# A three-layer recurrent scan as one unrolled stream at lags of 18 and 36 steps, with layer 0's input projections reading x in place

## What is computed

```
def step(h, x_t):                       # layer 0: gated
    fused = sigmoid(concat([x_t, h]) @ w_W + w_b)
    hidden_state, output_state = split(fused, 2)
    memory_state = x_t @ wx_W + wx_b + hidden_state * (h @ wh_W + wh_b)
    h_new = output_state * h + (1 - output_state) * tanh(memory_state)
x = x + layer0(x)                       # the scan over t gives h_1 .. h_512
x = x + layer1(x)                       # h_t = tanh(x_t @ Wx + b + h_{t-1} @ Wh)
x = x + layer2(x)                       # the same form
x = x + attention(x)                    # 16 heads, causal, an extra image token
```

## Time and profile before

| | us |
|---|---|
| median of 3 runs | 4057.07 |
| the profiled execution, own time | 4053.96 |
| its span in the trace | 4052.3 |
| TensorE busy | 3869.1 (95%) |
| VectorE busy | 2335.6 (58%) |
| ScalarE busy | 1066.0 (26%) |
| GpSimd busy | 159.7 (4%) |

### The profile page before, as it was taken

The page is one execution under the profiler, slowest core; times in us unless marked ns, Lnnn a source line. Parts: engine busy times, 40 slices in busy tenths (PEclk is TensorE's granted clock), DMA queues, the critical chain, the costliest instruction groups (busy, mean ns, idle before and its releaser), DMA issues. The chain is left out here.

```text
span 4052.3 us, 172362 instructions
## 1 busy us (share of the span) xinstructions
PE 3869.1 (95%) x78452; PEld 2600.6 (64%) x78452; DVE 2335.6 (58%) x8378; ACT 1066.0 (26%) x3931; POOL 159.7 (4%) x374
## 2 busy tenths in 40 slices
PE   6799999999999999999999999999769999999998
PEld 4577776777666699976666666775434555555555
DVE  3565665666566566656555665665325656665664
ACT  1121111111111111111111111111004555555555
POOL 0000000000000000000000000000000000000000
PEclk9999999999999999999999999999979999999999
DMA  5000000000000000000000000001000000000000
GB/s 188 3 4 4 3 3 3 3 3 3 4 3 3 3 4 3 3 4 3 3 4 3 3 3 3 3 3 65 2 6 1 12 9 12 14 12 12 14 7 19
DMA packets 34261, 46.85 MB, mean 12 GB/s; under 512 B 5819, under 2 KB 22251, under 8 KB 33526
## 3 DMA queue, kind: packets, MB, share of 16 engines
q1 hardware_dynamic: 31222, 29.43, 2.3%
q10 hardware_dynamic: 2304, 6.29, 0.4%
HBM read 27.33 MB, written 8.39 MB: 9 GB/s over the span
## 5 line engine op out<-in xcount | busy, mean ns | idle before, releaser
L181 PE MATMUL bank<-wh,h 128*8 128x256 f32 x16384 | 990.1, 381 | 62.1 <-DVE h L356 31.3
L201 PE MATMUL bank<-wh,h 128*16 128x256 f32 (+1 forms) x17408 | 997.1, 369 | 52.4 <-ACT h L237 50.7
L201 PEld LDWEIGHTS bank<-wh,h 128*16 128x16 f32 (+1 forms) x17408 | 529.3, 97 | 338.9 <-ACT h L237 73.5
L181 PEld LDWEIGHTS bank<-wh,h 128*8 128x8 f32 x16384 | 469.1, 90 | 390.7 <-DVE h L356 50.2
L328 DVE STREAM_TRANSPOSE tp<-bank 128x256 f32<-128x256 f32 x512 | 230.5, 450 | 643.0 <-PE bank L181 643.0
L187 PE MATMUL bank<-wh,h 128*8 128x128 f32 x16384 | 549.7, 274 | 0.0
L187 PEld LDWEIGHTS bank<-wh,h 128*8 128x8 f32 x16384 | 444.0, 90 | 117.7 <-issue 2.6
L250 ACT ACTIVATE gates_sb<-pre_sb 128x32 f32<-128x32 f32 x512 | 117.8, 230 | 1356.5 <-DVE pre_sb L330 1356.5
L225 PE MATMUL bank<-stage,w_qkv 128*32 128x128 f32 x11904 | 385.7, 273 | 0.0
L225 PEld LDWEIGHTS bank<-stage,w_qkv 128*32 128x32 f32 x11904 | 342.9, 110 | 44.1
L237 ACT ACTIVATE h<-sum 128x64 f32<-128x64 f32 (+1 forms) x544 | 138.1, 254 | 783.9 <-DVE sum L272 783.9
(11 more groups left out here) (132 smaller groups left out, 3326.6 us busy)
## 6 DMA issues: line engine op xcount, KB each, us to landing
xrows<-in_x_dram SPq DMA_DIRECT2D x32, 256.0 KB, 3.7
out_dram<-X SPq DMA_DIRECT2D x32, 256.0 KB, 2.6
w_qkv<-in_L_cond_c_attn_w_dram SPq DMA_DIRECT2D x1, 3072.0 KB, 18.1
wh<-in_L_cond_w_W_dram ACTq DMA_DIRECT2D x4, 512.0 KB, 8.8
w_qkv<-in_L_cond_w_W_dram ACTq DMA_DIRECT2D x4, 512.0 KB, 10.6
wx<-in_L_cond_Wx_dram SPq DMA_DIRECT2D x2, 1024.0 KB, 8.5
wh<-in_L_cond_Wh_dram SPq DMA_DIRECT2D x2, 1024.0 KB, 10.7
mask_all<-in_mask_Bx1x1xS_ff_dram SPq DMA_DIRECT2D x8, 256.0 KB, 3.2
```

The source lines that it names most:

```text
L181: mm = pe.matmul(mem.ps0[32 * j:32 * j + B, 0:2 * P], h0[:, us, k, ts, :], columns_of(mem.wh0[:, k, 0:3:2, :], j), start=(k == 0), stop=(k ...
L201: mm = pe.matmul(mem.ps12[32 * j:32 * j + B * len(ls), P * l0:P * l1], h12[:, us, k, ts, l0:l1, :].rearrange("p l b -> p (l b)"), columns_ ...
```

## The change

- The scan is one block with no loop and no barrier inside: 548 steps, of which 512 have layer 0. Layer 1 runs 18 steps behind layer 0, layer 2 36 behind (`LAG12`), so that the layers are at different places of their chunks.
- The states of layers 1 and 2 are kept in a ring of 32 steps. A chunk of 16 can wrap around its end and is then added in two pieces (`ring_parts`).
- In `pre12` the inputs of layers 1 and 2 lie at different t, so the one add becomes two.
- `fills_of(n)`: steps 0 and 1 of a round have two fills of layer 1, steps 2 and 3 two of layer 2, steps 4 to 15 one of layer 0 each.
- Layer 0's fills read X in place: the moving operand is 8 runs of 16 times, a sequence's 512 times apart. VectorE permutes when it keeps the result (`by_step`). GpSimd's copies are gone. VectorE's sum of X and a chunk of states now writes the stage tile of the next layer; only the last layer's sum writes X.
- `setup` loads, turns and copies only the 8 tiles of the first 128 times, and loads the projection weights ahead of the recurrent ones; the bias rows follow the first four tiles. The other 24 tiles come in during the scan, one a step from step 2: SyncE loads, TensorE turns it after the step's fills, ScalarE copies it before the gates of the next step.
- `add_last_chunk` is gone; the last sum is done by VectorE in the scan's block. The attention itself is the same.

```
-ROUNDS = NCH + 4
+LAG12 = [CH + 2, 2 * (CH + 2)]
+STEPS = T + LAG12[1]
+HR = 2 * CH
+TILES = [(b, tc) for tc in range(T // P) for b in range(B)]
+EARLY = B
+TILE_STEP = 2
...
+def fills_of(n):
+    m, t = divmod(n, CH)
+    if t < 2 and 0 <= m - 1 < NCH:
+        return [(1, m - 1, 2 * t + g) for g in range(2)]
+    if 2 <= t < 4 and 0 <= m - 2 < NCH:
+        return [(2, m - 2, 2 * (t - 2) + g) for g in range(2)]
+    if t >= 4 and m + 1 < NCH:
+        return [(0, m + 1, t - 4)]
+    return []
+def sum_of(n):
+    m, t = divmod(n, CH)
+    layer = {0: 0, 2: 1, 4: 2}.get(t)
+    if layer is not None and 0 <= m - 1 - layer < NCH:
+        return layer, m - 1 - layer
+    return None
...
+            for n in range(STEPS):
+                if n < T:
+                    main0(n)
+                if layers_of(n):
+                    main12(n)
+                if fills_of(n):
+                    fills(n)
+                if tile_of(n) is not None:
+                    turn_tile(tile_of(n))
...
                     for k in range(KC):
+                        rows = stage[layer - 1][:, c % 2, k, :] if layer else x_chunk(c)[:, k]
                         for j in range(KC):
                             at = g * P + 32 * j
                             mm = pe.matmul(mem.fillps[n % 2][32 * j:32 * (j + 1), f * N:(f + 1) * N],
-                                           w[:, k, at:at + 32], stage[layer][:, k, :],
+                                           mem.wx[layer][:, k, at:at + 32], rows,
...
+                for l in ls:
+                    ins = nc.vector.tensor_tensor(mem.sum12[:, l, :, :], turned[:, l, :, 0:B],
+                                                  xw12[:, l, at[l] // CH % 2, :, at[l] % CH, :], ALU.add)
+                ins.then_inc(s.pre12, 1)
...
+                    ins = nc.vector.tensor_scalar(
+                        dst, by_step(layer, mem.fillps[n % 2][:, f * N:(f + 1) * N]),
...
+            for n in range(STEPS + 1):
+                if n and layers_of(n - 1):
+                    pre12(n - 1)
+                if n and fills_of(n - 1):
+                    keep_fills(n - 1)
+                if sum_of(n) is not None:
+                    chunk_sum(*sum_of(n))
+                if n and n < T and n % CH == 0:
+                    dve.wait_ge(s.fill_kept, nfill[n])
+                if n < T:
+                    step0(n)
```

More of the change, by code:

```diff
@@ L47, with layers_of, counts, ring_parts @@
 NBIAS = _at
[L50 to L58, removed]
-    return out
[L62 to L82, removed]
+def layers_of(n):
+    return [l for l in range(2) if 0 <= n - LAG12[l] < T]
+def fills_of(n):
[13 more added lines that the diff above has]
+    return None
+def counts(per_step):
+    out = [0]
+    for n in range(STEPS + 1):
+        out.append(out[-1] + per_step(n))
+    return out
+def ring_parts(first):
+    slot = first % HR
+    head = min(CH, HR - slot)
+    return [(0, slot, head)] + ([(head, 0, CH - head)] if head < CH else [])
+def by_step(layer, columns):
+    return columns.rearrange("p (t b) -> p t b", b=B) if layer else columns.rearrange("p (b t) -> p t b", b=B)
 class Mem:
@@ L114, in scan_block @@
-def scan_block(nc, mem, sems, a, plans, steps, S, first, i):
-    s = sems
[L116 to L148, removed]
-    with nc.Block(no_gpsimd_drain=True) as block:
[L152 to L169, removed]
@@ L171, in _, with main0 @@
         @block.tensor
         def _(pe):
[L173 to L178, removed]
+            def main0(n):
+                if n:
+                    pe.wait_ge(s.h0_new, n)
+                state = h0_at(n - 1) if n else mem.h0_first
                 for k in range(KC):
@@ new lines, in _ @@
+            for n in range(STEPS + 1):
+                if n and layers_of(n - 1):
+                    tanh12(n - 1)
+                if n and tile_of(n - 1) is not None:
+                    i = tile_of(n - 1)
+                    b, tc = tiles[i]
+                    act.wait_ge(s.x_turned, i + 1)
+                    nc.scalar.copy(X[:, :, b, tc * P:(tc + 1) * P],
+                                   mem.xps[i % 2][:, :].rearrange("p (k t) -> p k t", k=KC)).then_inc(s.x_kept, 1)
+                if n < T:
+                    gates(n)
@@ L398, in setup @@
 def setup(nc, mem, sems, a):
     s = sems
-    NT = T // P
-    tiles = [(b, tc) for b in range(B) for tc in range(NT)]
+    tiles = TILES[:EARLY]
     loads = []
+    for k in range(KC):
+        rows = slice(k * P, (k + 1) * P)
+        loads.append((mem.wx[0][:, k, 0:2 * D], a["w_W"][rows, :]))
+        loads.append((mem.wx[0][:, k, 2 * D:3 * D], a["wx_W"][rows, :]))
+    FIRST = len(loads)
     for k in range(KC):
@@ L1109, in __init__ @@
         self.fill_kept = new("fill_kept")
-        self.chunk_op = new("chunk_op")
+        self.chunk_sum = new("chunk_sum")
+        self.layer_in = [new(f"layer{l}_in") for l in (1, 2)]
         self.rows_made = new("rows_made")
```

446 lines of the change are left out of this document (214 added, 232 removed).

## The result

The changed kernel takes 3947.71 us, the median of 4 runs (3945.37 to 3949.72), beside 4056.07 us of the kernel before (4 runs, 4054.74 to 4057.52). The ratio is 0.9728, with a 95% interval of 0.9714 to 0.9743: 2.7% faster, 5.7 us above the forecast of 3942 and inside the range. The profiled execution took 3949.72, its span is 3948.0 (before 4052.3, so 104.3 less).

A forecast was written before the change was run, and what follows sets the result against it. TensorE's order was taken to bound steps with all layers, the recurrence those with fewer. Terms -30, +27, -41.5, -69 and -1.4 sum to -115, taking 4053.96 to 3939; plus 3.1 gives 3942 us, range 3920 to 3985.

The forecast's parts named there:

- Start: Setup up to the first step: with only eight tiles ahead, first step at 34 instead of 64.07 us, -30.
- its upper end: Setup: if the 48 projection matmuls run at the slow early rate, they take 18 us, not 11; first step at 41.
- the 7 of my bound: Setup: upper side of the spread given for the first step's time, -5 to +7 us.
- Steps with layer 0: The 512 scan steps with layer 0: more run with all layers together, +27 us in sum.
- the +8: Scan: extra second fills in bound steps, and eight steps where a fill and a tile's transposes stand together, +8 us.
- Block changes: Seven block changes between steps with layer 0 vanish: four loop jumps at 8.5 us, three at 2.5, -41.5.
- rival C: Scan: slow instruction issue stalls the long stream as often as the loop did; 41.5 us stay, 3983; chance 0.08.
- Tail: Steps behind layer 0's last: 36 instead of 64, 102 us (60 with both layers, 42 with one) instead of 171, -69.
- End: Last sum: GpSimd's add with its block goes, VectorE's sum comes, -1.4 us.
- A (X at half rate): Layer 0's fills: TensorE reads X in runs of 16 at half rate, +305 us, 4247; chance 0.06.
- B (late VectorE): Scan: VectorE's sums double in length and exceed its spare time in step 4 of a round, +12 us, 3954; chance 0.08.

The follow-up runs named there:

- all tiles first: Changed kernel with all 32 tiles of x loaded and turned before the scan, none in it: 3970.08 us, ratio 0.9782.
- the unrolled loop: Kernel before with its loop written out, its nine blocks and their barriers kept: 4032.41 us, ratio 0.9946.
- the filler: Changed kernel with twelve useless matmuls behind main12 in each of the last 16 steps: 3941.96 us, ratio 0.9707.

## Why the prediction was right, point by point

The mechanisms were right and the sum of the spans was 10.7 us off (104.3 less against 115), nearly all of it at the start and in the tail. That the medians are only 5.7 apart is in part luck: to get from the profiled execution to the median, the working added the 3.1 by which they differed before, while the changed kernel's profiled execution stood 2.0 above its median.

**Start, forecast -30, measured -26.2.** The mechanism was right (all tiles first: 65.66). Two numbers of the working were off. Tile 3 went at 13.41, not at 12.2, since ScalarE began its table load at 11.38 and not 10.28, and the eighth tile came at 20.34, not within the 19.6 taken for all. And I took 12.5 from the projections to the first step as at full clock; it was 14.9, because they began at the lower rate. The working had named that as its upper end and the rule of the Trainium skill (TensorE: Matmul & The Clock Gate, "What's actually happening") beside it; trace and rule agree, by 2.4 us, which is a third of the 7 of my bound, since only the first three groups ran slow.

**Steps with layer 0, forecast 2737.4, measured 2737.2.** Steps are 5.20 and 6.07 from step 36 on; before, they are 4.49, but 5.22 in steps 32 to 35 with their two fills. The eight with a fill and a tile are 5.05, +0.56 each, inside the +8. Second adds, pieces and permuted keeps are hidden, as costed.

**Block changes, -41.5: right**, with 42.0 by the distances between steps. The four jumps gave 33.1 of the 34 forecast and the other three 8.9 of 7.5; the unrolled loop gained 25.6 against 24. What the working said of a jump was wrong in one point: rival C took the 3.60 us of L181 behind the wait for slow instructions, and it is the clock, granted at 0.50 there.

**Tail, forecast 102, measured 111.8.** This is the step that failed in size. With one layer I had 42 and it took 49.4 (2837.49 to 2886.84): I scaled the clock's price from the old 32 steps, 72 instead of 63.4. In those, fills stood three or four steps apart, and both times that the rate had fallen among them it came back beside a fill or right behind one, as the timeline of the kernel before shows (L225 is a fill):

```profile
2927.16 1.90 PE L201 MATMUL bank<-wh,h 128*8 128x128 f32 x32 [0.93 <-ACT h L237]
2928.83 1.93 PE L225 MATMUL bank<-stage,wx 128*32 128x128 f32 x32
2930.54 1.09 PE L201 MATMUL bank<-wh,h 128*8 128x128 f32 x32
```

Now the four fills stand in the first two steps, and 14 of the steps behind them are at 2.82: 14 x (2.82 - 1.99) = 11.6, which is what the filler gave back (11.7). When the rate falls varies with the same code: behind the second of the two steps with fills it held for two steps in the changed kernel, for six in the run with GpSimd copies, where the one-layer part took 45.7, and for nine behind the last fill of the kernel before. So an estimate of this term can be out by some 4 us whatever the working. With both layers I had 60 and it took 62.5 (2775.02 to 2837.49): two stalls for issue, 1.06 + 2.13, stand beside the 6 MB that I had called hidden. The loads are hidden from SyncE's side, but matmuls stood waiting for issue; with the loads later the same steps flow. The second add cost 0.07 a step (3.11 against 3.04), not 0.12.

**End, forecast -1.4, measured -3.8:** within what the attention varies by.

**Rivals.** A (X at half rate) is refuted by 273 ns from either source. B (late VectorE) is refuted: whole sums of 1.06 to 1.12, no wait for L359 behind the first steps. The Trainium skill's 2.5 ns a column (Vector Engine (DVE) Microarchitecture Reference, "Measured stream behaviour on trn2"), by which I had estimated 1.36 us, was measured with steps of 24 words and does not carry over: L321's sources step by 8 and by 16 words each element, and its 1.12 us over 512 columns is 2.2 ns with all fixed cost in it. C (the stalls stay) is refuted for the scan. Waits for issue did appear in the tail, where transfers of 6 MB run beside, and cost 3.2; that they have the same cause as the loop's is not shown.

## What to carry to other kernels

When a tuned stream still has gaps, cut the span where the regime changes and price each stretch by the distance between steps: here 104 us came from the start, block changes and the drain, and only 23 of them from TensorE's busy time. Shorter lags of a pipeline pay in its drain and cost in its body (more steps with all layers), so count both. A wait can cost more than its length: in the loop's waits of 5.4 to 5.9 us the granted clock fell to 1.2 GHz, and the step behind each took some 2.4 us more. Look at what the drain leaves to TensorE: half-busy steps there fell to 1.2 GHz, and a few useless matmuls in the waits, together with later bulk loads and more tiles in flight at the start, gave the fastest version of this study: 3931 to 3934 us, ratio 0.969.

## What the runs showed that I had not expected

- A fill whose moving operand is 8 runs of 16 float32, 512 apart, takes 273 ns a record, exactly as one contiguous run does. The keeps, of which layer 0's now permute, take 349 ns on average (L297), as they did before (L290).
- TensorE waited for issue (1.06 and 2.13 us) while 6 MB of loads moved, and did not when those loads started some steps later, though the same amount moved then as well. In the four other runs with short lags and early loads such waits were 0.23 to 0.68 and 1.10 to 1.58; in the two with long lags there were none.
- Filler of 12 matmuls in a step of 1.99 us, TensorE then waiting only 0.27, kept the granted clock at 1.00; without it TensorE waited 0.93 of 2.82 at the lower clock. In the setup 14 matmuls among waits of 0.2 to 1.5 did not keep it.
- A GpSimd copy of 512 columns stretched a VectorE add with two SBUF inputs from 0.23 to 0.64 and at most 0.995.
